# Weighing half of the experts' outputs on TensorE, and rearranged ends and beginnings of stages, in a four-layer decoder

## The reference

```python
# L1_ffn: one expert of 8 for each token, hidden width 1024
scores = jnp.einsum('bsh,he->bse', x, wr) + br
expert_id = jnp.argmax(scores, axis=-1)
h = jax.nn.gelu(jnp.einsum('bsh,ehf->ebsf', x, w1) + b1[:, None, None, :])
y = jnp.einsum('ebsf,efh->ebsh', h, w2) + b2[:, None, None, :]
out = jnp.einsum('ebsh,bse->bsh', y, one_hot)
...
# L2_ffn: two experts of 8 for each token, each weighed by its gate
for e in range(N_EXPERTS):
    ...
    h = jax.nn.relu(xe @ W1[e]) @ W2[e]
    y = y.at[idx].add(g[:, None] * h)
...
# L2_attn: gated linear attention, 16 heads of 64, decays from log_decay
log_decay = -jax.nn.softplus(x @ Wd.T + bd)
k_gated = k * jax.nn.sigmoid(x @ Wg.T)
s = exp(g) * s + k^T v;  o = q s          # a scan over the tokens
out = rmsnorm(o) * norm_w * jax.nn.sigmoid(x @ Wog.T) @ Wo.T
```

## Time and profile before

| | |
|---|---|
| time, 3 runs | median 2851.56 us (2849.23 to 2857.14) |
| profiled execution | 2857.49 us, of which the span is 2855.7 us |
| mean granted PE clock | 0.912 of full speed |
| instructions | 35241 |
| PE, DVE, ACT, POOL busy | 84%, 52%, 30%, 17% of the span |

### The profile page before, as it was taken

How to read it: one execution, slowest core, us unless ns; L and a number is a source line. 1 busy time by engine, 2 the same in 40 slices (tenths; PEclk the granted TensorE clock), 3 DMA queues, 4 the chain that set the end, 5 groups by cost and what they waited for, 6 DMA issues and landing times. The chain is left out here.

```text
span 2855.7 us, 35241 instructions
## 1 busy us (share of the span) xinstructions
PE 2403.9 (84%) x14043; PEld 1659.2 (58%) x14051; DVE 1479.7 (52%) x2541; ACT 857.6 (30%) x1223; POOL 488.7 (17%) x395
## 2 busy tenths in 40 slices
PE   5777775778888969967999998929999599999888
PEld 4665653432222758844667666826777367777674
DVE  8996866558774431125563654471011355545543
ACT  1111556434556122233432332202111132212132
POOL 3332330040000113310000001103221120000010
PEclk8988887988999979978999999859999699999999
DMA  3002000053340035622322231032231300000000
GB/s 109 0 1 86 19 11 20 7 128 84 62 65 22 13 126 208 228 99 78 94 63 63 63 94 32 8 120 78 100 100 50 104 17 17 17 12 17 1 32 30
DMA packets 71092, 177.13 MB, mean 62 GB/s; under 512 B 16519, under 2 KB 36488, under 8 KB 67305
## 3 DMA queue, kind: packets, MB, share of 16 engines
...
...
## 5 line engine op out<-in xcount | busy, mean ns | idle before, releaser
L1585 PE MATMUL L_ffn_h_ps<-L_ffn_xgT,L_ffn_w 128*128 128x512 f32 (+2 forms) x992 | 230.5, 388 | 3.3 <-DVE L_ffn_xgT L1642 1.4
L2233 PE MATMUL L_attn_X<-xT,L_attn_w 128*128 128x512 f32 x512 | 226.8, 595 | 0.0
L1596 PE MATMUL L_ffn_y_ps<-L_ffn_w,L_ffn_h 128*128 128x256 f32 x1008 | 223.0, 381 | 4.0 <-ACT L_ffn_h L1621 3.9
L525 DVE TENSOR_REDUCE L_attn_neg<-L_attn_Y 128x1 f32<-128x512 f32 (+3 forms) x304 | 187.3, 657 | 58.4 <-PE L_attn_Y L398 57.0
L1596 PEld LDWEIGHTS L_ffn_y_ps<-L_ffn_w,L_ffn_h 128*128 128x128 f32 x1008 | 189.7, 190 | 32.8 <-ACT L_ffn_h L1621 7.9
L1621 ACT ACTIVATE L_ffn_h<-L_ffn_h_ps,L_ffn_w 128x640 f32<-128x640 f32 (+2 forms) x184 | 101.5, 552 | 352.9 <-PE L_ffn_h_ps L1585 351.2
L1585 PEld LDWEIGHTS L_ffn_h_ps<-L_ffn_xgT,L_ffn_w 128*128 128x128 f32 x992 | 152.9, 191 | 80.2 <-issue 64.2
L495 ACT ACTIVATE L_attn_room<-L_attn_Y 128x1024 f32<-128x1024 f32 (+1 forms) x192 | 147.4, 812 | 82.6 <-PE L_attn_Y L449 82.0
L2233 PEld LDWEIGHTS L_attn_X<-xT,L_attn_w 128*128 128x128 f32 x512 | 94.7, 190 | 110.0 <-issue 108.1
L398 PE MATMUL L_attn_Y<-L_attn_K,L_attn_Q 104*128 104x512 bf16 (+3 forms) x384 | 120.8, 366 | 43.5 <-DVE L_attn_neg L525 25.1
L1651 DVE TENSOR_TENSOR L_ffn_yg<-L_ffn_y_ps,L_ffn_w 128x256 f32<-128x256 f32 x63 | 26.7, 425 | 223.2 <-PE L_ffn_y_ps L1596 223.2
...
## 6 DMA issues: line engine op xcount, KB each, us to landing
...
```

Source lines behind the costliest of these rows:

```text
L525: nc.vector.tensor_reduce(neg[:, c, j0:j0 + heads, tt], R[n % 2][:, 0:heads * width(tt, c)].rearrange("p (h k) -> p h k", h=heads), X_AXIS ...
L1585: ins = nc.tensor.matmul(h_ps[f % 2][:, lo // CW, 0:hi - lo], w1[g % NB][:, kt, f * P:(f + 1) * P], xgT[u][:, kt, lo:hi], start=kt == 0, s ...
L1596: ins = nc.tensor.matmul(y_ps[k % 2][:], h[:, f, t * P:(t + 1) * P], w2[g % NB][:, f, :], start=f == 0, stop=f == FT - 1)
L2233: ins = nc.tensor.matmul(x[:, c * CW:(c + 1) * CW], w[1 - par][:, kt, r, :], xT[:, kt, b * T + c * CW:b * T + (c + 1) * CW], start=kt == 0 ...
```

## The change

**Tails.** In L0_attn, L0_ffn and L1_attn the last batch (6, 7) becomes (6,) and (7,). In L0_xattn the last batch (12, 13, 14, 15) becomes (12, 13), (14,), (15,), and the turns of units 6 to 15 go in rotation to four banks of `S_ps`, which the scores no longer need then (argument `later`); some of them move ahead in `TURNS`, and the wait for `y_added` before `AFTER` is gone. In L2_attn and L3_attn DVE's last three norms stand each behind its unit's add, not behind all adds.

**Experts.** The odd units 1, 3, 5, 7 are no longer mixed by DVE. ACT makes diagonal matrices of their gates during the groups (`gates`: identity times the gate, 8 of 128x128 in L1_ffn, 16 in L2_ffn), and PE sums gate matrix times `got` and identity times x in PSUM (`weigh`). DVE takes the statistics of those units from PSUM, and the norm reads PSUM. POOL waits for its queue (`drain`) before the roots of the tail, where it did not before.

**First weights.** SP loads `wd`, `bd` and the first pair's `w` (640 KB) of L2_attn in the middle of L1_ffn, and the first `w` (384 KB) of L3_attn in the middle of L2_ffn (`FirstWeights`).

**L2_attn, turn -1.** ACT copies q in two halves first, and the copies free q's buffer; the gate, v and og follow, and the exponentials of the decays come last (`rise`). DVE makes `kT` before it works on `bc`, and `qd` from `qr`.

```diff
-            for u in range(NT // 2):
+            def weigh(u):
+                pe.wait_ge(sem["gates_made"], choices * len(weighed))
+                pe.wait_ge(sem["y_copied"], before[groups])
+                pe.wait_ge(sem["xg_copied"], before[groups])
+                pe.wait_ge(gathered[u], 16 * choices)
+                for n in tail.tiles(u):
+                    dst = tail.sums[u][:, n % 2, :]
+                    for c in range(choices):
+                        nc.tensor.matmul(dst, gates[:, c, weighed.index(n), :], got[:, c, n, :], start=c == 0, stop=False)
+                    ins = nc.tensor.matmul(dst, core.ident[:], core.x_tok[:, n, :], start=False, stop=True)
+                ins.then_inc(sem["summed"], 1)
+
+            weigh(1)
+            weigh(3)
+            tail.turn(pe, 0)
+            tail.turn(pe, 1)
+            weigh(5)
+            tail.turn(pe, 2)
+            tail.turn(pe, 3)
+            weigh(7)
+            for u in range(4, UNITS):
                 tail.turn(pe, u)
...
+                for k in range(max(0, g - 1) * PER, min(g * PER, choices * len(weighed))):
+                    c, i = k % choices, k // choices
+                    nc.scalar.activation(gates[:, c, i, :], core.ident[:], ACT.Copy,
+                                         scale=core.slot_gates[:, c, weighed[i]:weighed[i] + 1]).then_inc(sem["gates_made"], 1)
...
             for u in range(UNITS):
-                dve.wait_ge(gathered[u], 16 * choices)
-                for n in tail.tiles(u):
-                    mix(n)
-                dve.wait_ge(sem["mixed"], 2 * u + 2)
+                if u in tail.sums:
+                    dve.wait_ge(sem["summed"], u // 2 + 1)
+                else:
+                    dve.wait_ge(gathered[u], 16 * choices)
+                    for n in tail.tiles(u):
+                        mix(n)
+                    dve.wait_ge(sem["mixed"], u + 2)
                 tail.statistics(dve, u)
...
+            nc.gpsimd.drain()
             for b in range(len(tail.batches)):
                 tail.root(pool, b)
...
+            sp.wait_ge(sem["y_copied"], before[groups // 2])
+            following.load(sp)
...
-                    (tuple(range(8)), tuple(range(8, 12)), tuple(range(12, 16))))
-        ROOTS = {9: 0, 13: 1, 17: 2}
-        TURNS = {k: (k - 11,) for k in range(11, 17)} | {17: (6, 7, 8)}
-        AFTER = tuple(range(9, NT_))
+                    (tuple(range(8)), tuple(range(8, 12)), (12, 13), (14,), (15,)),
+                    later=(LATER, [S_ps[:, j, 0:KT * P].rearrange("p (k n) -> p k n", k=KT) for j in range(J)]))
+        ROOTS = {9: 0, 13: 1, 15: 2, 16: 3, 17: 4}
+        TURNS = {k: (k - 11,) for k in range(11, 16)} | {16: (5, 6, 7), 17: (8, 9)}
+        AFTER = tuple(range(10, NT_))
...
-                if has_next:
+                foremost = isinstance(n, int) and n == -1
+
+                def rise():
                     act.wait_ge(d_loaded[o], (half + par) * 64 + 64)
                     nc.scalar.activation(bp[o][:], bp[o][:], ACT.Exp).then_inc(bp_exp, 1)
...
+                if foremost:
+                    act.wait_ge(mm["q"], 1)
+                    nc.scalar.copy(qr[:, 0:CW], X[BUF["q"]][:, 0:CW]).then_inc(q_copied, 1)
+                    nc.scalar.copy(qr[:, CW:2 * CW], X[BUF["q"]][:, CW:2 * CW]).then_inc(read["q"], 1)
+                elif has_next:
+                    rise()
...
+                if foremost:
+                    rise()
```

More of the change, by code:

```diff
@@ L1106, in _ @@
                     tail.root(pool, ROOTS[n])
[L1107 removed]
+            for n in (NT_, NT_ + 1):
+                tail.root(pool, ROOTS[n])
 ROUND = 1.5 * 2.0 ** 23
@@ L2738, in _ @@
             pair_turns(dve, turn, 1)
-            for b in (1, 2, 3):
-                tail.norm(dve, b)
         @block.gpsimd
@@ L3358, in build @@
     ]
-    if first > 1:
+    if start > 1:
         with nc.Block() as block:
@@ L3363, in _ @@
                 clear_outputs(core, sp)
-    for n in range(first, last + 1):
+    for n in range(start, last + 1):
         if n == KEYS_FROM:
```

156 lines of the change are left out of this document (99 added, 57 removed).

## The result

| | before | changed |
|---|---|---|
| median, 4 runs each | 2850.65 us (2849.23 to 2857.14) | 2814.24 us (2809.76 to 2816.5) |
| profiled execution | 2857.49, span 2855.7 | 2809.76, span 2808.0 |
| mean granted PE clock | 0.912 | 0.928 |

The account below looks back on a forecast made before the run. PE was busy 84% of the span, but the change touches the seams between twelve stages, where every engine waits. The terms sum to -29.6 us, from the median 2851.56 to 2822; range 2808 to 2837.

Parts of the forecast that it names:

- Tail of L0_xattn: End of L0_xattn: last values 1.6 us earlier and a shorter chain behind the last statistics, -6.2 us; bounds -4 and -7.
- Tails of L0_attn, L0_ffn, L1_attn, L2_attn, L3_attn: Ends of these stages: smaller last batches or earlier norms shorten the last chain; -2.2, -2.0, -1.0, -0.7, -0.7 us.
- Start of L2_attn: First turn of L2_attn: earlier z and new order bring kv 15.6 us earlier, less 3 for low clock; -12.6 us.
- the cold price: First turn of L2_attn: PE starts kv at low clock after standing for 6 us, costing 3 us.
- The weighing: Tails of L1_ffn and L2_ffn: PE's queue, behind ACT's norms, replaces DVE as the bound; +2.4 and -0.4 us.
- the course that I chose: Experts' tails: weigh(1) and weigh(7) at half clock, weigh(3) at full; +2.4 us in L1_ffn, -0.4 in L2_ffn.
- the bound of -3.0: Tail of L2_ffn: the weighing's result if weigh(7) runs at full clock, -3.0 us; in L1_ffn the same case gives +0.7.
- The drain: Steps after L1_ffn and L2_ffn: POOL's early drain is covered and both fall to 0.9 us; -1.4 and -3.9 us.
- Rival C: Steps after the experts: the drain doesn't shorten them, the excess has another cause or comes back; 2827 us, chance 0.15.
- Start of L3_attn: First matmul of L3_attn: without the transfer of w, DVE's second memset is what is late next; -0.9 us.
- Rival B: Experts' tails and first turn of L2_attn: PE stays at half clock, the turn pays double; 2829 us, chance 0.17.
- Rival D: L2_attn: PE stands once in every turn and the clock falls each time; net +16 us or 2868, chance 0.03.

Follow-up runs that it names:

- banks: The changed kernel with the last four tiles of L0_xattn in one batch again, four banks and earlier turns kept; 2825.29 us, ratio 0.9891.
- busykv: The changed kernel with 11 matmuls of zeros on PE in its wait before the first kv of L2_attn; 2815.59 us, ratio 0.987.
- oldfirst: The changed kernel with the old order in the first turn of L2_attn, early loads kept; 2828.6 us, ratio 0.9922.
- beforedrain: The kernel before with only POOL's drain added ahead of the roots of both experts' tails; 2846.78 us against 2852.86, ratio 0.9979.
- nodrain: The changed kernel without POOL's drain before the roots of the experts' tails; 2822.4 us, ratio 0.9911.

## Why the prediction was right

Predicted 2822 us, a gain of 29.6; measured 2814.24, a gain of 36.4. The direction and most mechanisms stood; several terms were too small, and the clock in the long stretches between the seams, which the sum put at nothing, gave some more. Below, "measured" is the kernel before against the three profiled executions of the changed kernel, in the order of the table.

- *Tail of L0_xattn*, predicted -6.2, measured -8.0, -7.9, -7.2 by the stage. The last values came 3.3 us earlier, not the 1.6 that I took as half of a chain; what follows them was as worked out. The split is worth 1.6 of it (banks).
- *Tails of L0_attn, L0_ffn, L1_attn, L2_attn, L3_attn*, predicted -2.2, -2.0, -1.0, -0.7, -0.7. From the last statistics to the end of the last copy it was 6.1, 5.6, 4.4, 4.1 and 4.1 us before, and 3.5 to 3.9, 3.5 to 3.7, 3.6, 3.5 and 3.5 after: as predicted. In L0_attn the step to the next stage grew by 0.4. L1_attn as a stage lost 3.1 to 4.8; what goes beyond its 0.9 isn't the tail's.
- *Start of L2_attn*, predicted -12.6. The end of the first turn, the first out, came 15.0, 12.6 and 14.2 us earlier. kv came 17.6, 15.4 and 15.7 us earlier where the prediction had 15.6, and kv and s1 together took 6.3, 6.6 and 5.3 us instead of 3.8, so the cold price is 2.5, 2.8 and 1.5, where I took 3. Dummies in the wait take it away (busykv: 3.8). In the first execution kv came earliest because z ran at full clock there, 1.5 us shorter; I had z at half clock in both kernels. oldfirst puts the reordering at 10 to 12 us at the first out.
- *Behind the first turn of L2_attn* the stage lost another 4.9, 4.8 and 2.7 us, of which 0.7 is the tail. The sum had nothing for it. The step between the halves, 58.4 us before and 56.8 after, is 1.6 of it, but it is 56.8 in beforedrain too, so it isn't the change's.
- *The weighing*, predicted +2.4 in L1_ffn and -0.4 in L2_ffn. Measured +0.9, +3.6 and +3.7, by the clock of that execution, and -1.8, -2.1 and -1.7. PE's queue and clock took DVE's place, as predicted. But the course that I chose (weigh(1) and weigh(7) cold, weigh(3) warm) ran in none of the three: weigh(7) was at full clock each time. The first execution is near the bound that I had named for that, +0.7; in the other two weigh(3) in part and most of weigh(5) were cold, and the last turns too. That the sum is close to the chosen +2.4 on average is luck. In L2_ffn half or more of weigh(5) was cold and weigh(7) warm in all three, and the result lies between the sum and the bound of -3.0. The norm of the last unit from PSUM, for which I added nothing, took 0.99 us for two and not 0.73, within the bound of 0.3.
- *The drain*, predicted -1.4 and -3.9. Measured -1.4 and -4.0 in the trace, -6 us alone (beforedrain) and +8.5 when it is left out (nodrain). Rival C falls.
- *Start of L3_attn*, predicted -0.9: measured -0.92, released by the memset named as next. With the tail that is 1.6 of the 5.1 us that the stage lost; the rest goes with the clock at its end, as shown above.
- *Rival B*, a PE that stays cold: true in part. Two of three executions come near its +4.1 in L1_ffn, but never with weigh(7) cold, not in L2_ffn, and the first turn of L2_attn never paid double. *Rival D*, a fall in each turn: the turns stand 27.2 us apart in both kernels, so it falls.

The terms of the sum, as they came out, add up to some 37, 32 and 32 us less in the three executions, where the prediction had 29.6. The profiles are 48, 46 and 47 us apart, the medians 36, 38 and 41. The difference lies in L1_attn, in L2_attn behind its first turn, in L3_attn and, in two of the three, in L1_xattn, in places that the change doesn't touch. So the centre of the forecast was too slow by some 8 us: a part of that is L0_xattn's 1.8, L2_ffn's 1.4 and up to 2.4 in the first turn of L2_attn, and the other part was not foreseen at all.
